# Small per-mode values of a long-filter stage held on 128 partitions of 32 instead of 32 partitions of 128

## The reference, cut to what matters

```python
dt = exp(log_dt)                          # [64]
Cc = C[..., 0] + 1j * C[..., 1]           # [64, 64]
A = -exp(log_A_real) + 1j * A_imag        # [64, 64]
dtA = A * dt[:, None]
Ct = Cc * (exp(dtA) - 1.0) / A            # the small per-mode values
K = 2.0 * einsum('hn,hnl->hl', Ct, exp(dtA[:, :, None] * arange(1024))).real
y = irfft(rfft(x, 2048) * rfft(K, 2048)[None], 2048)[..., :1024] + x * D[:, None]
y = y * mask                              # by the lengths
out = x + ffn(y)                          # gate, up [2752, 1024], down [1024, 2752], fake-quantised
```

## Time and profile before

| | us |
|---|---|
| median of 3 runs | 1300.58 |
| lowest, highest | 1298.82, 1306.31 |
| the profiled execution | 1303.45 |
| its span, first to last instruction | 1301.0 |
| busy: PE, DVE, ACT, POOL | 1245.1, 922.0, 408.5, 338.3 |

### The profile page before, as it was taken

One profiled execution on the slowest core, in us unless ns is written; L12 is line 12 of the kernel. 1 busy time (PEld: TensorE's weight loads), 2 busy tenths in 40 slices (PEclk: granted clock), 3 DMA queues, 4 the chain that ended last, 5 costly groups with the idle time before them and its releaser, 6 DMA issues.

```text
span 1301.0 us, 19748 instructions
## 1 busy us (share of the span) xinstructions
PE 1245.1 (96%) x6676; PEld 675.0 (52%) x6676; DVE 922.0 (71%) x1542; ACT 408.5 (31%) x595; POOL 338.3 (26%) x318
## 2 busy tenths in 40 slices
PE   2699999998989999999999999999999999999997
PEld 0577777766754444444444444444444444444443
DVE  7789988887867676566777556777656677656675
ACT  2444454544532222222222222222222222222222
POOL 2233344334521111222111212211222211122210
PEclk9999999999999999999999999999999999999999
DMA  3499999989952232232333233233223333223322
GB/s 101 141 276 269 290 288 294 274 270 261 302 201 69 54 84 70 62 71 71 72 83 79 62 71 70 69 79 87 62 67 70 73 79 80 69 62 71 72 64 77
DMA packets 137737, 161.51 MB, mean 124 GB/s; under 512 B 101660, under 2 KB 101870, under 8 KB 136430
## 3 DMA queue, kind: packets, MB, share of 16 engines
q1 hardware_dynamic: 137710, 161.16, 45.8%
HBM read 113.28 MB, written 25.49 MB: 107 GB/s over the span
## 4 chain that ended last, share of the span: by engine, by line
PE 83%; DVE 6%; DMA 5%; issue 3%; SPq 1%; ACT 1%; POOL 1%; DVEq 0%; POOLq 0%; ACTq 0%
PE bank L1054 46%; PE bank L1082 22%; PE bank L844 10%; DMA chunk<-in_x 3%; PE bank L830 1%; PE bank L861 1%; DVE tail L790 1%; DMA rows<-xq_dram 1%; PE bank L1089 1%; DVE tail L768 1%; DVE tail L794 1%; DMA rows<-in_x 1%; POOL w_int L628 1%; DVE w_max L735 0%; ACT wide L666 0%
## 5 line engine op out<-in xcount | busy, mean ns | idle before, releaser
L1054 PE MATMUL bank<-wgu,rows 128*128 128x512 bf16 (+1 forms) x3072 | 602.2, 358 | 5.7 <-DMA rows<-xq_dram 5.7
L1054 PEld LDWEIGHTS bank<-wgu,rows 128*128 128x128 bf16 x3072 | 291.6, 98 | 315.7 <-issue 9.2
L1120 DVE SCALAR_TENSOR_TENSOR chunk<-bank,sx_all,wide 128x512 f32<-128x512 f32 (+1 forms) x288 | 198.5, 707 | 257.6 <-PE bank L1054 257.5
L1230 POOL TENSOR_TENSOR w_int<-chunk,rounder 128x512 bf16<-128x512 f32 x186 | 174.4, 952 | 698.4 <-ACT chunk L1193 689.1
L1187 ACT ACTIVATE chunk<-chunk 128x512 f32<-128x512 f32 x192 | 112.3, 585 | 598.1 <-DVE chunk L1120 598.1
L1082 PE MATMUL bank<-wd,tail 128*128 128x512 bf16 x1346 | 296.1, 379 | 0.0
L844 PE MATMUL bank<-chunk 128*128 128x512 f32 (+7 forms) x1024 | 263.3, 410 | 1.7 <-ACT s_rows L716 0.9
L844 PEld LDWEIGHTS bank<-chunk 128*128 128x128 f32 x1024 | 176.2, 191 | 87.1 <-issue 54.4
L1082 PEld LDWEIGHTS bank<-wd,tail 128*128 128x128 bf16 x1346 | 131.1, 98 | 151.9 <-issue 1.1
L628 POOL TENSOR_TENSOR w_int<-wide,rounder 128x1024 bf16<-128x1024 f32 (+1 forms) x68 | 134.4, 1986 | 221.5 <-ACT wide L660 164.7
L1193 ACT ACTIVATE chunk<-chunk,h_inv 128x512 f32<-128x512 f32 x192 | 118.4, 664 | 80.4 <-DVE h_inv L1141 80.4
(11 more groups left out here) (137 smaller groups left out, 594.0 us busy)
## 6 DMA issues: line engine op xcount, KB each, us to landing
chunk<-k_rev SPq DMA_DIRECT2D x64, 512.0 KB, 6.9
tail<-in_x SPq DMA_DIRECT2D x64, 256.0 KB, 3.8
out_x<-tail SPq DMA_DIRECT2D x64, 256.0 KB, 3.2
wide<-in_L_ffn_w_gate SPq DMA_DIRECT2D x22, 512.0 KB, 6.9
wide<-in_L_ffn_w_up SPq DMA_DIRECT2D x22, 512.0 KB, 8.5
wide<-in_L_ffn_w_down SPq DMA_DIRECT2D x8, 1376.0 KB, 8.2
rows<-in_x SPq DMA_DIRECT2D x32, 256.0 KB, 6.8
chunk<-in_x SPq DMA_DIRECT2D x32, 256.0 KB, 7.1
```

What stands on the lines that cost most here:

```text
L1054: last = pe.matmul(bank[:, 0:n], xq[:, par, c, :], wgu[:, NC - 1 - c, first + cols.start:first + cols.stop], start=(c == 0), stop=(c == NC ...
L1120: dve.scalar_tensor_tensor(out=buf[j % 2][:, 0:n], in0=bank[:, 0:n], scalar=sx, in1=s[:, cols], op0=ALU.mult, op1=ALU.mult).then_inc(gu_sc ...
L1230: pool.tensor_tensor(h_int[:, piece(j)], h[:, par, piece(j)], rounder[:].to_broadcast([P, n]), ALU.subtract).then_inc(h_int_ready, 1)
```

## The change

The three large inputs are loaded to 32 partitions as before, but into staging tiles. log_dt is loaded to all 128 partitions (all 64 channels' values on each, 256 bytes a partition, where it was two values on each of 32). PE turns A_imag, the two halves of C and log_A_real by four transposes as soon as they and `ident` are there; DVE copies the 128x128 result out of PSUM. From there `small` has 22 planes of 128 partitions by 32. The exponential runs over 96 elements (32 of log_A_real, 64 of log_dt) where it ran over 130. Scaling by dt becomes an elementwise product with a strided slice of the exponential, for 64 partitions at a time, where it was a multiplication by a per-partition scalar. The transposes and the copy that stood behind line 274 go, and the tables read the planes directly. On POOL the two selects that finish `ident` and `last_one` move ahead of the long memset of `d_rows`. PE's matmuls with D wait for line 248's copy where they waited for line 274.

```diff
@@ tiles @@
-    logs = sb([H2, P + 2])
-    a_im = sb([H2, P])
-    c_in = sb([H2, P, 2])
-    e_n = sb([H2, P + 2])
...
-    cols = sb([P, 4, H2])
+    log_rows = sb([H2, P])
+    a_rows = sb([H2, P])
+    c_rows = sb([H2, P, 2])
+
+    cols = sb([P, 4 * H2 + H])
+    a_im, c_re, c_im = (cols[:, k * H2:(k + 1) * H2] for k in range(3))
+    logs = cols[:, 3 * H2:4 * H2 + H]
+    e_n = sb([P, H2 + H])
...
-    small = scratch[0:H2, 6 * size:6 * size + 22 * P].rearrange("p (k n) -> p k n", k=22)
+    small = scratch[:, 6 * size:6 * size + 22 * H2].rearrange("p (k n) -> p k n", k=22)
...
-        return cols[:, k, :].unsqueeze(2).to_broadcast([P, H2, R])
+        return s(k).unsqueeze(2).to_broadcast([P, H2, R])
@@ on_sync @@
-        sp.dma_start(logs[:, 0:P], log_A_real.rearrange("(a b) n -> a (b n)", b=2)).then_inc(loaded, 16)
-        sp.dma_start(logs[:, P:P + 2], log_dt.rearrange("(a b) -> a b", b=2)).then_inc(loaded, 16)
-        sp.dma_start(a_im[:], A_imag.rearrange("(a b) n -> a (b n)", b=2)).then_inc(loaded, 16)
-        sp.dma_start(c_in[:], C.rearrange("(a b) n two -> a (b n) two", b=2)).then_inc(loaded, 16)
+        sp.dma_start(log_rows[:], log_A_real.rearrange("(a b) n -> a (b n)", b=2)).then_inc(loaded, 16)
+        sp.dma_start(logs[:, H2:H2 + H], log_dt.rearrange("(a h) -> a h", a=1).to_broadcast([P, H])).then_inc(dt_loaded, 16)
+        sp.dma_start(a_rows[:], A_imag.rearrange("(a b) n -> a (b n)", b=2)).then_inc(loaded, 16)
+        sp.dma_start(c_rows[:], C.rearrange("(a b) n two -> a (b n) two", b=2)).then_inc(loaded, 16)
@@ on_vector @@
-        dve.wait_ge(loaded, 64)
+        dve.wait_ge(in_turned, 1)
+        tick(dve.tensor_copy(cols[:, 0:4 * H2], ps_cols[:]))
+        dve.wait_ge(dt_loaded, 16)
...
-            step = e_p[:, P + hp:P + hp + 1]
-            tick(dve.tensor_scalar(small[:, A, half], small[:, A_RE, half], step, None, ALU.mult))
-            tick(dve.tensor_scalar(small[:, BB, half], a_im[:, half], step, None, ALU.mult))
+            step = e_p[half, H2 + hp:H2 + H:2]
+            tick(dve.tensor_tensor(small[half, A, :], small[half, A_RE, :], step, ALU.mult))
+            tick(dve.tensor_tensor(small[half, BB, :], a_im[half, :], step, ALU.mult))
...
+            reached["d_row"] = count[0]
...
-        reached["small"] = count[0]
-
-
-        dve.wait_ge(cols_done, 1)
-        tick(dve.tensor_copy(cols[:], ps_cols[:]))
...
@@ on_gpsimd @@
+        pool.wait_ge(const_step, 2)
+        pool.affine_select(out=ident[:], ...).then_inc(ident_ready, 1)
+        pool.affine_select(out=last_one[:], ...)
         pool.memset(d_rows[:], 0.0)
...
@@ on_tensor @@
+        pe.wait_ge(ident_ready, 1)
+        pe.wait_ge(loaded, 48)
+        for k, rows in enumerate((a_rows[:], c_rows[:, :, 0], c_rows[:, :, 1], log_rows[:])):
+            last = pe.transpose(ps_cols[:, k * H2:(k + 1) * H2], rows, ident[0:H2, 0:H2])
+        last.then_inc(in_turned, 1)
         pe.wait_ge(consts_ready, 1)
-        pe.wait_ge(dve_step, reached["small"])
-        for k, src in enumerate((A, FRAC, CT_RE, CT_IM)):
-            last = pe.transpose(ps_cols[:, k, :], s(src), ident[0:H2, 0:H2])
-        last.then_inc(cols_done, 1)
+        pe.wait_ge(dve_step, reached["d_row"])
```

More of the change, by code:

```diff
@@ L107, in sem @@
         return ctx.enter_context(nc.semaphore(name))
-    logs = sb([H2, P + 2])
-    a_im = sb([H2, P])
-    c_in = sb([H2, P, 2])
-    e_n = sb([H2, P + 2])
-    e_r = sb([H2, P + 2])
-    e_p = sb([H2, P + 2])
-    e_bits = sb([H2, P + 2], I32)
-    cols = sb([P, 4, H2])
+    log_rows = sb([H2, P])
[5 more added lines that the diff above has]
+    e_n = sb([P, H2 + H])
+    e_r = sb([P, H2 + H])
+    e_p = sb([P, H2 + H])
+    e_bits = sb([P, H2 + H], I32)
     power = sb([P, 2, R])
@@ L134, in long_filters @@
     power_i = sb([P, 2, R], I32)
-    ps_cols = banks[7][:, 0:4 * H2].rearrange("p (k h) -> p k h", k=4)
+    ps_cols = banks[7][:, 0:4 * H2]
     HB = 512 // R
@@ L143, in long_filters @@
     len_loaded = sem("len_loaded")
+    dt_loaded = sem("dt_loaded")
+    ident_ready = sem("ident_ready")
+    in_turned = sem("in_turned")
     const_step = sem("const_step")
@@ L149, in long_filters @@
     pool_small = sem("pool_small")
-    cols_done = sem("cols_done")
     act_decay = sem("act_decay")
@@ L226, in on_vector @@
                                       op0=ALU.add, op1=ALU.mult))
-        tick(dve.tensor_scalar(s(A_RE), e_p[:, 0:P], -1.0, None, ALU.mult))
+        tick(dve.tensor_scalar(s(A_RE), e_p[:, 0:H2], -1.0, None, ALU.mult))
         reached["real"] = count[0]
@@ L274, in on_vector @@
         tick(dve.tensor_tensor(s(CT_IM), s(CT_IM), s(T0), ALU.add))
-        reached["small"] = count[0]
-        dve.wait_ge(cols_done, 1)
-        tick(dve.tensor_copy(cols[:], ps_cols[:]))
         for kind in range(2):
-            tick(dve.tensor_tensor(decay[:, kind], over(0), powers[:, kind], ALU.mult))
+            tick(dve.tensor_tensor(decay[:, kind], over(A), powers[:, kind], ALU.mult))
         reached["decay"] = count[0]
@@ L285, in on_vector @@
             for kind in range(2):
-                tick(dve.tensor_tensor(phase[:, kind, hs], over(1)[:, hs], powers[:, kind, hs], ALU.mult))
+                tick(dve.tensor_tensor(phase[:, kind, hs], over(FRAC)[:, hs], powers[:, kind, hs], ALU.mult))
             tick(dve.tensor_scalar(turns[:, :, hs], phase[:, :, hs], ROUND, ROUND, ALU.add, ALU.subtract))
@@ L300, in on_vector @@
             t0, t1 = turns[:, 0, hs], turns[:, 1, hs]
-            tick(dve.tensor_tensor(t0, si[:, 0], over(3)[:, hs], ALU.mult))
-            tick(dve.tensor_tensor(t1, co[:, 0], over(2)[:, hs], ALU.mult))
+            tick(dve.tensor_tensor(t0, si[:, 0], over(CT_IM)[:, hs], ALU.mult))
+            tick(dve.tensor_tensor(t1, co[:, 0], over(CT_RE)[:, hs], ALU.mult))
             tick(dve.tensor_tensor(high_re[:, hs], t1, t0, ALU.subtract))
-            tick(dve.tensor_tensor(t0, co[:, 0], over(3)[:, hs], ALU.mult))
-            tick(dve.tensor_tensor(t1, si[:, 0], over(2)[:, hs], ALU.mult))
+            tick(dve.tensor_tensor(t0, co[:, 0], over(CT_IM)[:, hs], ALU.mult))
+            tick(dve.tensor_tensor(t1, si[:, 0], over(CT_RE)[:, hs], ALU.mult))
             tick(dve.tensor_tensor(high_im[:, hs], t1, t0, ALU.add))
@@ L311, in on_gpsimd @@
         pool.memset(last_one[:], 0.0).then_inc(const_step, 1)
+        pool.wait_ge(const_step, 2)
+        pool.affine_select(out=ident[:], in_=ident[:], compare_op=ALU.not_equal, fill=1.0, base=0,
+                           pattern=[[-1, P]], channel_multiplier=1).then_inc(ident_ready, 1)
+        pool.affine_select(out=last_one[:], in_=last_one[:], compare_op=ALU.not_equal, fill=1.0,
+                           base=-(R - 1), pattern=[[1, R]], channel_multiplier=0)
         pool.memset(d_rows[:], 0.0)
@@ L320, in on_gpsimd @@
         pool.iota(place_i[:], [[P, NC]], base=P - 1, channel_multiplier=-1)
[L321 to L326, removed]
+        pool.wait_ge(ident_ready, 1)
         pool.tensor_copy(identb[:], ident[:]).then_inc(consts_ready, 1)
-        pool.wait_ge(loaded, 64)
         pool.wait_ge(dve_step, reached["real"])
[L331 to L334, removed]
+        for out, left, right in ((NORM, s(A_RE), s(A_RE)), (N_IM, a_im, a_im),
+                                 (W_RE, c_re, s(A_RE)), (C0, c_im, a_im),
+                                 (W_IM, c_im, s(A_RE)), (C1, c_re, a_im)):
             pool.tensor_tensor(s(out), left, right, ALU.mult).then_inc(pool_products, 1)
```

## The result

| | before | changed |
|---|---|---|
| median, us (7 runs each) | 1301.13 | 1294.9 |
| lowest to highest | 1298.82 to 1306.31 | 1292.49 to 1298.75 |
| ratio, 95% interval | | 0.9948 (0.9929 to 0.9968) |
| span of the profiled execution | 1301.0 | 1292.5 |

The changed kernel is faster by 0.52%, 6.8 us by the ratio (4.2 to 9.2), where 4.4 us (0.34%) was forecast. A second set of 11 runs of the same kernel gave 0.9961 (0.9941 to 0.9981), 5.1 us. Both intervals hold the forecast.

The account below looks back on a forecast made before the run. Ahead of the first convolution the kernel was taken to stand on DVE's serial list. Savings 0.39 + 0.20 + 1.18 + 1.38 + 1.50 - 0.05 - 0.15 = 4.45, say 4.4 us, off 1300.58 gave 1296.2, range 1291.5 to 1301.5.

Parts of the forecast that it names:

- exponential and line 228: Head of DVE's list: exponential from 130 to 96 elements saves 0.39 us, line 228 from 128 to 32 saves 40 ns.
- ten instructions beside POOL: DVE's lines 233 to 69, running beside POOL's nine: 1.50 us saved, between 0.38 and 1.88.
- line 237 to 256: DVE's stretch before the tanh is needed, including one reciprocal: from 3.49 to 2.68 us.
- line 256 to 274: End of DVE's small list, a reciprocal and two-input instructions at 32 elements: 1.91 us saved.
- transposes and copy moved: 1.17 us goes at the list's end and returns at the head; the strided read of C costs 0.05.
- C's landing: Head: log_dt's load to 128 partitions, ahead of C, delays C by 0.15 us, at worst 1.4.
- the disturbance: DVE's slowing beside POOL in lines 233 to 69: 1.50 us before, a quarter, 0.38, expected after.
- An instruction at 32 elements: DVE's small list: a two-input instruction takes 188 ns at 32 elements, against 280 before at 128.
- The rest as a block: From line 282 on all moves forward unchanged; line 282 to the first Toeplitz load's landing stays 27.07 us.
- That the disturbance stays: Rival: DVE and POOL hinder each other per instruction, still costing 1.5 us; saving 3.3, time 1297.3 us; chance 0.15.
- the transfer stage takes the start back: Rival: transfers from 70 to 330 us don't start earlier, so the end stays at 1300.6 us; chance 0.12.
- The two lucks: Rivals, transfer stage: six further late x waits, 1304.4 us, chance 0.07; or three waits vanish, 1292.1 us, chance 0.12.

Follow-up runs that it names:

- Experiment 3: Changed kernel with log_dt's load issued behind C's: C lands 1.7 us after issue, tables at 18.63 us, ratio 0.9955 to the kernel before.
- Experiments 9 and 10: 9: kernel before, POOL's nine instructions over 32 columns: line 68 284 ns. 10: changed kernel, nine more 128x128 POOL products: DVE's 32-element instructions 312 to 327 ns.
- experiments 1, 2 and 5: 1: changed kernel delayed by six DVE products, ratio 0.9999. 2: kernel before without 13 small DVE instructions, 0.9969. 5: changed kernel without the same 13, 0.9956.
- 17.93: Changed kernel, log_dt loaded behind C, two casts ahead of the wait for turned inputs, lengths' cast and mask behind the tables: ratio 0.9965.
- 17.51: The kernel with tables at 17.93, plus log_dt's load issued by ACT and the tanh ahead of the sines: ratio 0.9957.

## Why the prediction was right, step by step

The place and the mechanism held: the tables start earlier, nothing new stands on the path, the rest moves as a block. The terms, forecast against trace, in us saved:

| step | forecast | measured | how read |
|---|---|---|---|
| exponential and line 228 | 0.43 | 0.39 | 8.86 - 3.86, now 10.25 - 5.64 |
| ten instructions beside POOL | 1.50 | 1.83 | 12.93 - 8.86, now 12.49 - 10.25 |
| line 237 to 256 | 0.81 | 0.80 | 16.42 - 12.93, now 15.18 - 12.49 |
| line 256 to 274 | 1.91 | 1.80 | 22.19 - 16.42, now 19.15 - 15.18 |
| transposes and copy moved | -0.05 | 0.09 | 1.17 + 0.02 of wait, now 5.64 - 4.54 |
| C's landing | -0.15 | -0.70 | 3.84, now 4.54 |
| sum | 4.45 | 4.21 | 23.36 - 19.15 |

The strided read of C cost nothing that can be seen: four transposes take 0.61 as before. The tanh, costed at nothing with 0.55 us to spare, ended at 14.38 us, 0.80 ahead of line 264. That the sum came within 0.24 us of the trace is in part luck: C's landing was 0.55 worse than forecast, the disturbance 0.33 and the transposes 0.14 better.

- **C's landing** was sized wrongly. I argued from engines that were busy for 0.07 of the time and took 0.15 between 0 and 1.4. Experiment 3 shows 0.7: the 128 pieces are short work for the DMA engines as a whole and still stand ahead of C. It lies in the middle of the bounds, and the choice near the lower one had no row behind it.
- **The disturbance** was priced per element of DVE, a quarter of 1.50. Experiments 9 and 10, one execution each, show that POOL's length decides it; beside POOL's instructions of 32 elements DVE lost some 0.04 us over the ten. The gain was near the upper end that I had written down, 1.88. The Trainium skill (SBUF — State Buffer, SBUF: two separate sides) says that one of the two engines holds the shared port pair for its whole instruction and the other blocks. Beside POOL's products of 128x128 the two went one for one at 0.35 us, as taking turns would have it, and the prediction's argument that DVE did not block was weaker than it looked. But the step isn't the sum of the two: POOL's products alone would have to take 0.13 us, and they are 398 ns long. Beside POOL's instructions of 32 elements the rule isn't to be seen: DVE's took 181 to 204 ns there.
- **An instruction at 32 elements** came to 191 ns, where I had taken 188. Here the Trainium skill's (N+151)/0.96 (VectorE: DVE Perf Modes, the section on the TRN2 errata), 190.6 ns, agrees to the nanosecond for 128 partitions; it is above the rows for 32 partitions (280 against 290.6).
- **The rest as a block.** From line 282 to the landing of the first Toeplitz load it was 27.07 us and is 27.32; 0.25 went, of which 0.08 is the load itself and the rest lies between PE's first products and the stores. After that the lead stays at 3.95 for six turns.
- **The rivals.** That the disturbance stays is refuted. That the transfer stage takes the start back is refuted as a whole by experiments 1, 2 and 5. The two lucks, late x transfers, vary from one execution to the next: PE's waits for the x of the turns (`chunk<-in_x`) between 45 and 395 us were 4.1 us in the kernel before, 1.9 and 4.0 in two executions of the changed one, and 1.9 to 6.0 in all ten. They don't go with the start of the tables. The prediction had no term for the clock, which weighed more in these executions.

The predicted 1296.2 us stands against 1294.9 and 1295.65 in the two sets. I gave 0.70 to a change within 0.5% and 0.25 to more; the sets gave 0.52% and 0.39%. What lies above 4.2 us in the first set, 2.6 us, has no cause that any experiment showed. The clock is part of it: the mean of that set's granted clocks is 0.9957, and 0.995 in the runs of the kernel before, which at 1.4 us for 0.001 is about 1 us. The rest lies within the interval, which reaches down to 4.2; that it is spread is argued, not shown. That 1296.2 us stands only 1.3 us from 1294.9, though the saving was 2.4 us larger than forecast, is partly luck too: the kernel before came out at 1301.13 and not at the 1300.58 that the forecast was set against.

None of the three better starts (18.63, 17.93, 17.51) gave a time that can be told from the changed kernel's. The last one keeps no wait between the inputs and the tables and is the one I would keep, on the strength of its rows, not of its ratio.

## What to carry to other kernels

A shorter serial list of small instructions ahead of everything paid nearly one for one here; count its instructions times the step of that shape, and expect only the length above some 150 ns (the fixed part of these fp32 instructions) to shrink when the same values are laid on more partitions. A change that gathers data on all partitions adds small DMA pieces: look who waits behind them, whichever engine issues them. When a kernel's runs spread by 0.6% and a change is worth 0.3%, shift the start by known amounts in both kernels and read the line with each execution's granted clock beside it, since one comparison of two profiles mixes the change with late transfers and clock drops that come and go in the same program.

## What the runs showed of the hardware that was not expected

- DVE is slowed by POOL according to POOL's length: 312 to 327 ns beside 128x128 products, 181 to 204 beside 128x32 ones, for the same instructions of 32 elements; and one DVE instruction took 1019 ns, not 289, beside a POOL memset of 32x640.
- 128 pieces of 256 bytes, issued 0.9 us ahead of C or by another engine at the start, delayed its landing from 1.7 to 2.4 and 2.5 us, with the DMA engines busy for a tenth of the first 4 us (0.10 and 0.11).
- The same sixteen matmuls at the start of the convolution took 4.21 us at a granted clock of 1.00 in one execution and 6.39 at 0.65 in another of the same program. Over the ten profiled executions the time at 1.2 GHz in the second part went from 3.4 to 17.1 us.
